# A mixture-of-experts stage listed by choice, with a scatter of gated rows in place of a final sum

## The reference, cut to what matters

```python
B, S, D, F, E = (1, 4096, 512, 256, 8); K = 2
logits = xf @ router_w
gate_vals, idx = jax.lax.top_k(logits, K)
gates = jax.nn.softmax(gate_vals, axis=-1)
for e in range(E):
    h = relu(xf @ w1[e] + b1[e]) @ w2[e] + b2[e]
    y = layernorm(xf + h, gamma[e], beta[e])
    w = sum(where(idx == e, gates, 0.0), axis=-1)
    out = out + w[:, None] * y
result = x3 + out          # x3: the rows before the last normalisation
```

## Time and profile before

| | us |
|---|---|
| median of 3 runs | 3298.16 |
| the profiled execution, its own time | 3299.97 |
| its span | 3298.2 |
| PE / DVE / ACT / POOL busy over the span | 2704.4 / 2567.3 / 1697.4 / 2061.7 |
| slot loop, end of the first `down` to end of the last | 2874.3 to 3199.8 |
| final sum, last `outer` to the end of the span | 3203.9 to 3298.2 |

### The profile page before, as it was taken

The page is one execution under the profiler, slowest core; times in us unless marked ns, Lnnn a source line. Parts: engine busy times, 40 slices in busy tenths (PEclk is TensorE's granted clock), DMA queues, the critical chain, the costliest instruction groups (busy, mean ns, idle before and its releaser), DMA issues. The chain is left out here.

```text
span 3298.2 us, 51851 instructions
## 1 busy us (share of the span) xinstructions
PE 2704.4 (82%) x11877; PEld 1690.8 (51%) x11877; DVE 2567.3 (78%) x5131; ACT 1697.4 (51%) x5677; POOL 2061.7 (63%) x2092
## 2 busy tenths in 40 slices
PE   6987888871888888885999999997999997799970
PEld 6544444440333333332556555567888885466640
DVE  8776666651999999998999999995656563589874
ACT  5222222210665666665999999983343342355540
POOL 2777777776777777776777777752212220288876
PEclk8888888875999999998999999997999998899995
DMA  4554555544888888887777877863111112633338
GB/s 168 195 188 167 172 175 177 167 159 157 264 263 259 262 265 263 263 262 221 228 230 233 233 230 230 232 184 115 46 54 51 51 52 88 234 114 114 118 109 286
DMA packets 241127, 600.41 MB, mean 182 GB/s; under 512 B 51649, under 2 KB 60737, under 8 KB 235970
## 3 DMA queue, kind: packets, MB, share of 16 engines
q0 software_dynamic: 120832, 345.92, 35.9%
q1 hardware_dynamic: 120002, 251.18, 22.0%
HBM read 485.62 MB, written 111.32 MB: 181 GB/s over the span
## 5 line engine op out<-in xcount | busy, mean ns | idle before, releaser
L1273 PE MATMUL at_pair<-wide,hot_t 128*128 x1152 | 581.1, 620 | 114.2 <-ACT hot_t L1124 101.2
L1322 PE MATMUL at_pair<-product,v_hot 128*128 128x260 f32 x2304 | 617.0, 401 | 50.0 <-DVE product L1072 21.9
L362 POOL DMA_INDIRECT records<-staged,address x544 | 540.1, 993 | 180.5 <-issue 161.6
L912 POOL DMA_INDIRECT fetched<-t_v,at_index x504 | 478.6, 950 | 199.4 <-issue 74.6
L902 POOL DMA_INDIRECT fetched<-t_k,at_index x504 | 481.3, 955 | 154.9 <-issue 103.6
L1322 PEld LDWEIGHTS at_pair<-product,v_hot 128*128 128x128 f32 x2304 | 394.8, 190 | 267.2 <-issue 158.8
L658 PE MATMUL qkv_prod<-wide 128*128 128x512 f32 x768 | 397.0, 680 | 91.0 <-ACT wide L402 82.9
L1064 DVE TENSOR_TENSOR wide<-at_pair,wide 128x520 f32 x576 | 400.8, 696 | 14.6 <-issue 10.2
L1273 PEld LDWEIGHTS at_pair<-wide,hot_t 128*128 128x128 f32 x1152 | 186.5, 189 | 374.1 <-issue 370.1
L991 DVE TENSOR_TENSOR product<-at_pair,fetched 128x512 f32<-128x512 f32 x504 | 342.9, 683 | 27.3 <-DMA fetched<-t_k,at_index 20.7
L1132 ACT ACTIVATE product<-product 128x64 f32<-128x64 f32 x864 | 215.9, 250 | 279.0 <-DVE product L991 277.5
(11 more groups left out here) (312 smaller groups left out, 4740.6 us busy)
## 6 DMA issues: line engine op xcount, KB each, us to landing
row_bc<-in_src SPq DMA_DIRECT2D x34, 1024.0 KB, 5.4
pair_rows<-kept_v SPq DMA_DIRECT2D x72, 260.0 KB, 4.1
by_slot<-m_y SPq DMA_DIRECT2D x72, 256.0 KB, 2.0
low_bc<-low_row SPq DMA_DIRECT2D x34, 512.0 KB
wide<-in_x SPq DMA_DIRECT2D x64, 256.0 KB, 3.7
kept_v<-pair_rows SPq DMA_DIRECT2D x36, 260.0 KB, 3.9
kept_v<-at_shared SPq DMA_DIRECT2D x36, 260.0 KB
records<-staged,address POOLq DMA_INDIRECT x544, 2.8
```

The lines of the kernel that those rows point to most:

```text
L362: eng.indirect_dma_start(records, bass.IndirectOffsetOnAxis(address[:, b, u:u + 1], 0), staged[:, b, u, :], None,).then_inc(put[b][u], 16)
L912: eng.indirect_dma_start(fetched[:, n % SLOTS, :], None, v, bass.IndirectOffsetOnAxis(index[:, t:t + 1], 0)).then_inc(s_row[n % SLOTS], 16)
L1273: nc.tensor.matmul(q_edge[u % 4], hot_t[:, g % 2, u % BATCH * P:(u % BATCH + 1) * P], q_sb[:, bass.ds(at, 1), :].rearrange("p a c -> p (a ...
L1322: last = nc.tensor.matmul(pair[u % 3][:, n, 0:HALF], hot[:, u % 4, :], product[:, u % 4, n * HALF:(n + 1) * HALF], start=True, stop=True)
```

## The change

- The experts' rows are listed twice: first all first choices (39 slot tiles, 32 + 7), then all second choices (39), 78 in all.
- `out_and_ffn` stores x3 itself and z (instead of z, mean, deviation) in rows of 1028 floats: x3, 2 spare, z, 2 for the gates. The last two are written from ACT when the gates are known, as 4096 pieces of 8 bytes, and the gathers wait for that. A second small write (4096 pieces of 8 bytes, spare columns) is on SP's queue early in `out_and_ffn`.
- In the slot loop a first-choice tile is gathered whole (4112 bytes a row), gets x3 + g1·y1 in place of x3, and is scattered whole to a second array `summed` by an indirect DMA of POOL. A second-choice tile is gathered from `summed` (4112 bytes a row) and scattered to `out` (2048 bytes a row). Slots without a row are dropped by the bounds check. There is no final sum and no `by_slot`.
- The first five second-choice tiles (`LATE_PARTS`) gather z from `t_z3` ahead, and their partial row (x3 + g1·y1) late, once the scatters of all first-choice tiles have landed; DVE adds it after its gain instead of before.
- b2 is cut into three bf16 parts on DVE, sent through memory, and added on PE by a bf16 product of ones (3 rows deep) with the parts before `down` (`down_bias`). The loads of a b2 broadcast and POOL's L1993 and L2010 are gone; ACT scales beta by the gate; DVE adds the partial row (`add_base`) and multiplies 1/deviation by the gate (128x1).
- The loop's tiles start on separate semaphores per weight, DVE works out the gates before it lists, and counting is in bf16.

```diff
             def store(t, m):
+                r_x3.wait(eng, t, m)
+                eng.dma_start(rows(z3[:, 0:C], t, m), base[:, t % 2, m, :]).then_inc(put_x3.sem(m), 16)
                 r_z3.wait(eng, t, m)
-                eng.dma_start(rows(z3, t, m), row_block(t, m, ZROW)).then_inc(put_z3.sem(m), 16)
+                eng.dma_start(rows(z3[:, PART:PART + C], t, m), row_block(t, m, C)).then_inc(put_z3.sem(m), 16)
...
-                if n:
-                    nc.vector.tensor_copy(row_block(t, m, ZROW, C), mean_var[:, 1, m, :])
...
-    SLOTS = TOP * T + E
+    EACH = T + E - 1
+    SLOTS = TOP * EACH
...
+            def gather(n):
+                u = n % TURN
+                if n >= TURN:
+                    e_done.wait(eng, 0, n - TURN)
+                    if not second(n - TURN):
+                        wait_put(eng, n - TURN)
+                if late(n):
+                    if n == EACH:
+                        eng.wait_ge(s_ready, 2)
+                    eng.indirect_dma_start(rows_sb[:, u, PART:], None, z3_parts, ...).then_inc(got[u], 16)
+                else:
+                    if second(n):
+                        all_put(n)
+                    eng.indirect_dma_start(rows_sb[:, u, :], None, summed if second(n) else z3, ...).then_inc(got[u], 16)
...
+            def late_part(n):
+                all_put(n)
+                eng.indirect_dma_start(rows_sb[:, n % TURN, 0:PART], None, summed_parts, ...
+                                       ).then_inc(moved_part[n - EACH], 16)
...
+            eng.wait_ge(s_ready, 1)
+            eng.wait_ge(s_gate_home, 16)
+            for n in range(LEAD):
+                gather(n)
+            for n in range(SLOTS):
+                if n + LEAD < SLOTS:
+                    gather(n + LEAD)
+                if n:
+                    scatter(n - 1)
+                if late(n):
+                    late_part(n)
+            scatter(SLOTS - 1)
...
+            eng.wait_ge(s_gate, 1)
+            nc.scalar.dma_start(z3.rearrange("(t p) w -> p t w", p=P)[:, :, PART + C:], gate[:, :, :]).then_inc(s_gate_home, 16)
...
+            def outer(n, e):
+                e_base.wait(eng, 0, n - 2)
+                nc.scalar.activation(base[:, n % 2, :], flat(beta_sb[:, e, :]), ACT.Copy, scale=row_gate(n))
...
+            def add_base(n):
+                e_outer.wait(eng, 0, n)
+                if late(n):
+                    eng.wait_ge(moved_part[n - EACH], 16)
+                nc.vector.tensor_tensor(acc[:, n % 2, :], rows_sb[:, n % TURN, 0:C], base[:, n % 2, :], ALU.add
+                                        ).then_inc(e_base.sem(n), 1)
...
+            def outer(n):
+                to = mine if second(n) else rows_sb[:, n % TURN, 0:C]
+                nc.vector.scalar_tensor_tensor(to, mine, root[:, n % 2:n % 2 + 1], acc[:, n % 2, :], ALU.mult, ALU.add
+                                               ).then_inc(e_done.sem(n), 1)
...
+            for n in range(SLOTS):
+                wait_rows(eng, n)
+                spread(n)
+                if n:
+                    outer(n - 1)
+                if not late(n):
+                    add_base(n)
+                gain(n, e)
+                if late(n):
+                    add_base(n)
...
+            def down_bias(n, e):
+                e_y.wait(eng, 0, n - 2)
+                nc.tensor.matmul(down_ps[n % 2][:, :], ones_b[0:PARTS, :], flat(b2_sb[:, e, :]), start=True, stop=False)
```

More of the change, by code:

```diff
@@ L1435, in _ @@
         def _(eng):
-            put_z3.start(eng)
+            for r in (put_z3, put_x3):
+                r.start(eng)
             def load(t, m):
@@ new lines, in _, with columns @@
+            for k in range(TOP * LIST_TURNS):
+                r_tile_hot.wait(eng, 0, k)
+                nc.scalar.activation(tile_id[:, k % 2, 0, :, :, :], tile_hot[:, k % 2, :, :, :], ACT.Copy, scale=row_id[:, 0:1]
+                                     ).then_inc(r_hot_p.sem(k), 1)
+            eng.wait_ge(s_ready, 1)
+            def columns(n):
+                e_turn.wait(eng, 0, n)
+                e_up.wait(eng, 0, n - 2)
+                nc.scalar.copy(zT[:, n % 2, :], turned[n % 2][:, :]).then_inc(e_zT.sem(n), 1)
@@ L2082, in _ @@
-            hidden(0, 0)
-            hidden_columns(0, 0)
-            def body(i, more):
-                for u in range(TURN):
-                    if u < TURN - 2 or more:
-                        columns(i, u + 2)
-                    if u < TURN - 1 or more:
-                        hidden(i, u + 1)
-                        hidden_columns(i, u + 1)
-                    e_var.wait(eng, i, u)
-                    e_done.wait(eng, i, u - 2)
-                    nc.scalar.activation(root[:, u % 2:u % 2 + 1], mean_var[:, 1:2], ACT.Sqrt, bias=eps[:, :]).then_inc(e_root.sem(u), 1)
-                    if u < TURN - 1 or more:
-                        outer(i, u + 1)
@@ L2153, in _ @@
-            st.link(nc.vector.tensor_tensor(slot[:, :, :], begun[:, 0:T, :], within.rearrange("p (t e) -> p t e", e=E), ALU.add))
-            st.link(nc.vector.tensor_tensor(slot[:, :, :], slot[:, :, :],
-                                            start[:, :].unsqueeze(1).broadcast_to([P, T, E]), ALU.add))
-            for c in range(TOP):
-                st.link(nc.vector.tensor_tensor(first[:, :, :], slot[:, :, :], one[:, c, :, :], ALU.mult))
-                st.link(nc.vector.tensor_reduce(place[:, c, :], first[:, :, :], AX.X, ALU.add))
@@ L2240, in _ @@
+            outer(SLOTS - 1)
         @block.tensor
@@ new lines, in _ @@
+            chosen = one[:, :, :, :].rearrange("p c e t -> p (c e t)")
+            nc.tensor.matmul(within[:, :], not_after[:, :], chosen, start=True, stop=True)
+            nc.tensor.matmul(total[:, :], ones_b[:, :], chosen, start=True, stop=True).then_inc(s_counted, 1)
+            for k in range(TOP * LIST_TURNS):
+                r_hot.wait(eng, 0, k)
+                r_hot_p.wait(eng, 0, k)
+                c, i = divmod(k, LIST_TURNS)
+                for m in range(CHUNK):
+                    g, t = divmod(m, 2)
+                    last = nc.tensor.matmul(list_ps[c], part_hot[:, k % 2, g, :, t], tile_id[:, k % 2, :, g, :, t],
+                                            start=(i == 0 and m == 0), stop=(i == LIST_TURNS - 1 and m == CHUNK - 1))
+                last.then_inc(r_listed.sem(k), 1)
```

603 lines of the change are left out of this document (292 added, 311 removed).

## The result

The changed kernel takes **3307.59 us**, the median of 20 runs (3302.0 to 3313.87), against 3300.34 for the kernel before (20 runs, 3296.37 to 3304.24): ratio 1.0023, 95% interval 1.0016 to 1.003. The forecast was 3249.8 with a range of 3226 to 3284, so it was wrong by 58 us and on the wrong side. The profiled execution took 3307.92 us, 8.0 more than that of before (3299.97), and its span 3306.2.

A forecast was written before the change was run, and what follows sets the result against it. The slot loop was taken as PE's 4.19 us a tile plus 0.4 from POOL's additions delaying DVE, the final sum as DMA-bound. −94.3 + 18.7 + 21 + 2 + 4.2 = −48.4 us gave a median of 3249.8 us, range 3226 to 3284.

The forecast's parts named there:

- Final sum, −94.3: End of the kernel before: the stretch from the last `outer` to the end disappears, −94.3 us.
- The turn, p = 4.47: Slot loop: p, time per tile, 4.47 us against 4.58, PE and gather (landing L 5.2) binding together; 77 turns, +18.7 us.
- The bf16 product, 0.27: Slot loop: the three-row product for b2 adds 0.27 us to PE's turn, between 0 and 0.27.
- Seam, +21: Between first-choice and second-choice lists: waits for scatters and late gathers add 21 us, bounds 12 and 28.
- Start, +2: Start of `experts`: first gather waits for the gates' small write (17 to 32 us, taken 22), +2 us, bounds −4 and +12.
- `out_and_ffn`, 0: Block before `experts`: PE is busy 96.6 us of 100, so two more stores and a small copy change nothing.
- Rival D: Start of `experts`: writes of 8 bytes go at half pace, gates land near 2882, all engines wait; 3270 us, chance 10%.
- End, +4.2: Loop's end: a last scatter follows `outer`, with release, landing, 0.3 us to the end and gate product, +4.2 us.
- PE's clock, priced at nothing: Behind the seam: PE's clock may fall under 1.00 while half idle; priced at nothing since PE has time to spare.
- Rival A: Slot loop: the gather is late, L (its landing) = 6.5 us, p = 4.88, +31.6 us; 3281 us, chance 18%.
- Rival B: Slot loop: POOL's DMA issues hold DVE off, 0.65 us each, DVE's turn 5.3 us; 3314 us, chance 8%.
- Rival C: Loop and seam: product half hidden, p = 4.30, PE keeps its lead (12 us), start gains 2; 3224 us, chance 14%.

The follow-up runs named there:

- e2: The changed kernel with gathers five tiles ahead instead of four and six late parts instead of five: 3284.95 us, ratio 0.9953.
- e4: The changed kernel with gathers five tiles ahead, six late parts and no bf16 product of b2 (b2 left out of the result): 3252.74 us, ratio 0.9855.
- e1: The changed kernel without the bf16 product of b2 (b2 left out of the result), gathers four tiles ahead: 3302.45 us, ratio 1.0004.
- e7: The kernel before with one more indirect gather by POOL at its end, waited for until it lands: 3308.31 us, ratio 1.002.
- e11: e7 with a bounds check on the indices of the extra last gather: 3308.96 us, ratio 1.0024.
- e5: e2 with all six late parts issued together in the turn of the first: 3264.04 us, ratio 0.9883.
- e6: e5 with the six late parts issued three, two and one in the first three turns of the second list: 3263.16 us, ratio 0.9883.

## Why the prediction was wrong

- **Final sum, −94.3.** Right: it is gone, and the whole difference lies in what was to come in its place.
- **The turn, p = 4.47: the step that failed.** The mechanism was right: there are two loops, PE's and the gather's through POOL's queue, and e2 and e4 show both. Three terms were too small. *Release to issue*: I wrote 0.1 us, which I took from nowhere in the trace; it is 0.81 beside a busy DVE and 0.79 at the idle end (3295.74 to 3296.53). The rows of the kernel before had it: the loop's first gather starts 0.83 us behind POOL's own copy of its index, and in the chain of waits the sum's first gather waits for the last store (rows below): landed at 3205.96, issued at 3206.84. *The scatter's issue*: 0.94 us, taken from gathers of the final sum; it is 1.40 in the loop, where DVE's gain (L2237) is running when the issue starts, and 0.98 for the last one, when DVE had nothing left to do. *PE's part behind the landing*: 4.3, 5.43 where PE has waited; 0.56 of the difference is the copy on ACT, which then lies bare, and some 0.3 the new product. Together 0.7 + 0.46 + 1.1 = 2.3 us on three turns, against p ≥ 4.45 that is 5.1 to 5.2. That the measured terms give back the measured 5.09 and 4.88 is a fit after the fact; the test is e2. Cost: 38·0.62 + 33·0.41 = 37 us. From the chain of waits of the kernel before (start us, us, what):

```profile
3203.96 2.00 DMA by_slot<-m_y
3205.96 0.02 issue
...
3206.12 0.72 issue
3206.84 0.96 POOL m_rows L2029
```

- **The bf16 product, 0.27.** It costs 0.41 to 0.42 where PE binds (e2 against e4). With four gathers ahead e1 got 5 us back, part of the gain being lost to PE's clock.
- **Seam, +21.** Five waits of DVE, 6.3 and 4.8 to 5.7 us: 51.2 − 6·4.47 = 24.3. Right, inside 12 to 28. Above PE's own 4.61 it is 23.5.
- **Start, +2.** +2.6, but that is luck. The gates landed in 18.4 us, at the near end of 17 to 32, and the first gather came 0.4 us earlier than before, not 2 later; the further read per small piece that the prediction priced at some 20 us is not to be seen. The 3.0 us came behind the gather, where the sum had no term.
- **`out_and_ffn`, 0.** It became 4.0 us shorter with two more stores and the small write in it; why, no run shows. Rival D is out, since the gates landed in 18.4 us and not in 42.
- **End, +4.2.** It became about +11. The release took 0.7 more, DVE 0.6 more, and the span ends 7.9 us after the last packets, not 0.3 after the landing. e7 and e11 show 5.7 us of that on the kernel before. A like stretch stands in the trace of before: the sort block ends behind POOL's indirect DMAs, the last of them issued from 788.27 to 789.23, and the next block begins at 798.56.
- **The unchanged blocks, 0.** +12.3 us. No step of the prediction had them, and the sum could not have.
- **PE's clock, priced at nothing.** In the changed kernel's seam DVE's waits for late parts stand beside it and cover it. Where they are gone it costs 2.0 us (e5, and 1.8 in e6), and without the product it took some 0.3 us a tile of the first list (e1).
- **Rival A**, the late gather (18%), is the one that came true in kind: p = 4.88 in the second half, as A had it with L = 6.5, but with L at 4.2 to 5.0 and the delay ahead of the landing. In the first half it was 5.09.
- **Rival B** is false, although it gave the nearest number (3314). The single lines of `outer` in the kernel after (duration ns min/median/max):

```profile
L2246 DVE SCALAR_TENSOR_TENSOR m_rows<-m_y,m_root,m_z_cols x39: 750/751/753, 2891.6 to 3085.2; 128x512 f32<-128x512 f32 x39
L2246 DVE SCALAR_TENSOR_TENSOR m_y<-m_y,m_root,m_z_cols x39: 750/751/753, 3095.7 to 3295.0; 128x512 f32<-128x512 f32 x39
```

  Not one of 78 is longer than 753 ns beside two indirect issues per turn. The part of it that is true is the other direction: DVE holds POOL's issue up (1.40 us).
- **Rival C** needed PE to keep its lead; its p of 4.30 was below PE's own 4.61.

The sum was −48.4; with the measured lengths it is −94.3 + 56 (loop: 405.7, less 325.5, less the seam's 24) + 24 + 3 + 11 = 0 for the block, and 8 more come from outside it: 12.3 less 4.0.

## What to carry to other kernels

When a loop passes through an in-order queue, write down every term of it from a row, the release to issue too, and compute how far a small error in each moves the period: here 2.3 us too little on three turns cost 37 of the 48 us that were missing. When two loops come out equal, as here at 4.46 and 4.45, the forecast is not safe at all; change the lead by one and one of them drops out, which was worth 22.6 us here. Put a transfer that waits for nothing new ahead of the ones that wait for the tile at hand: 20.9 us more in the seam. And where a wait leaves PE idle, price the slower clock behind it: it costs nothing only as long as another wait covers it.

## What was not expected of the hardware

- An indirect DMA of POOL that had to wait starts some 0.8 us behind its release, whoever releases it: 0.81 us behind DVE in the loop, 0.79 at the idle end, 0.83 behind POOL's own copy, 0.88 behind a store's landing (3205.96 to 3206.84). Behind another indirect DMA, with nothing to wait for, it starts after 0.30.
- An indirect issue that starts while a DVE operation with two SBUF inputs is running takes 1.40 us in the median (1.07 to 1.43; 72 in the changed kernel from 2875 us on); the scatter at 2965.22 overlaps L2237, which ends at 2965.74. All 84 others take 0.94 to 1.03 us, scatters too, and also beside L2220, which has one input in PSUM. It is not the scatter: the one gather that was hit, at 3175.83, took 1.34. DVE itself is not held off (750 to 753 ns). The Trainium skill (SBUF — State Buffer, section Who interferes with whom) says that a software DMA stalled by a DVE operation was starved of port time for its descriptors. The trace agrees that the issue is held up, by 0.4 us; that port time is the reason it does not show. The prediction had used only the other direction, DVE held off by the issue, and there the trace agrees too.
- A one-pass product with a depth of three rows, ahead of the fp32 group of `down` into the same PSUM tile, adds 0.41 to 0.42 us per tile, where 48 such products in a row took 0.27 each.
- A span that ends right behind an indirect DMA of POOL has 7.3 to 7.9 us of silence behind the last packets, and 1.6 behind a store of SP.
- The issue of the same indirect DMA takes 10 (records), 12 (K) and 17 ns (V) more in the changed kernel. The means for K are 965 to 971 ns in all nine profiles of the changed kind and 955 to 958 in the four of the other. Over 1552 issues that is 20 us of POOL; the two blocks are 12.3 us longer. Neither the order of the tensors, nor the length of one, nor five more semaphores, nor a bound on the indices does it.
- PE's granted clock falls where PE waits, and the work behind the wait pays for it. In the seam, PE half idle, it was 0.86, and an `up` group of 1.89 us took 3.40 and 3.17 at the seam's first two tiles; beside the waits for late parts that cost nothing. In e5 a single idle stretch of 4.58 us was followed by 3.5 us at 0.52 and cost 2.0 us. In e1 less work per tile brought 0.93 over the first list instead of 1.00.
